# Sixteen transposes of a head in one stretch, and scores two pairs ahead instead of three, in an attention pipeline

## What is computed

```python
q, k, v = (split_heads(x @ w + b) for w, b in ((wq, bq), (wk, bk), (wv, bv)))
scores = einsum('bhqd,bhkd->bhqk', q, k) * dh ** -0.5 + adj[:, None]
ctx = einsum('bhij,bhjd->bhid', softmax(scores, -1), v)
x1 = rmsnorm(x + ctx @ wo + bo, alpha1, gamma1)
x2 = rmsnorm(x1 + silu(x1 @ w1 + b1) @ w2 + b2, alpha2, gamma2)
out = layernorm(x + x2)
```

## Time and profile before

| | before |
|---|---|
| median of 3 runs | 1987.84 us (1987.14 to 1990.58) |
| the profiled execution: its time, its span | 1988.0 us, 1986.0 us |
| busy share PE, PEld, DVE, ACT, POOL | 97%, 86%, 67%, 59%, 34% |
| mean granted TensorE clock | 0.988 |
| transposes of probabilities (L655), count, mean | 2048, 273 ns |
| `pT_hi` (L449) and `pT_lo` (L540), count, mean | 256 each, 1026 and 1225 ns |
| exponentials (L442), count, mean | 512, 712 ns |
| logits on `adj_s` (L532), count, mean | 448, 687 ns |

### The profile page before, as it was taken

One profiled execution on the slowest core, in us unless ns is written; L12 is line 12 of the kernel. 1 busy time (PEld: TensorE's weight loads), 2 busy tenths in 40 slices (PEclk: granted clock), 3 DMA queues, 4 the chain that ended last, 5 costly groups with the idle time before them and its releaser, 6 DMA issues. The chain is left out here.

```text
span 1986.0 us, 35712 instructions
## 1 busy us (share of the span) xinstructions
PE 1931.9 (97%) x10336; PEld 1703.9 (86%) x10336; DVE 1334.3 (67%) x2270; ACT 1173.4 (59%) x1896; POOL 675.2 (34%) x796
## 2 busy tenths in 40 slices
PE   7999999999999999999966999999999999999998
PEld 5888888888888888888855999999999999999997
DVE  5777777777777777777756656565666555656644
ACT  4877778777787777877745433444443344444432
POOL 2000000000000000000015667766667666566643
PEclk9999999999999999999987999999999999999999
DMA  7655565555655556455633311222221122222011
GB/s 228 146 142 151 154 181 132 142 150 155 181 130 143 149 155 183 126 145 149 158 114 106 110 60 58 81 84 84 84 83 50 44 77 84 84 84 84 18 39 40
DMA packets 107363, 226.86 MB, mean 114 GB/s; under 512 B 15041, under 2 KB 43457, under 8 KB 105281
## 3 DMA queue, kind: packets, MB, share of 16 engines
q1 hardware_dynamic: 107328, 226.43, 39.4%
HBM read 108.93 MB, written 41.94 MB: 76 GB/s over the span
## 5 line engine op out<-in xcount | busy, mean ns | idle before, releaser
L540 DVE TENSOR_TENSOR pT_lo<-ps_t,pT_hi 128x1024 fp32r<-128x1024 f32 x256 | 313.6, 1225 | 143.9 <-ACT pT_hi L449 143.9
L449 ACT ACTIVATE pT_hi<-ps_t 128x1024 fp32r<-128x1024 f32 x256 | 262.6, 1026 | 179.0 <-PE ps_t L655 177.6
L379 POOL TENSOR_TENSOR xT_lo<-xT_raw,xT_hi 128x512 fp32r<-128x512 f32 x48 | 62.3, 1300 | 853.0 <-ACT xT_hi L428 853.0
L442 ACT ACTIVATE probs<-probs,neg_max 128x512 f32<-128x512 f32 x512 | 338.9, 712 | 5.1 <-DVE neg_max L532 5.1
L532 DVE CUSTOM_DVE_ANT_0 probs<-ps_s,adj_s 128x512 f32<-128x512 f32 x448 | 291.0, 687 | 39.7 <-PE ps_s L646 32.6
L1129 DVE TENSOR_TENSOR h_lo<-hidden,h_hi 128x512 fp32r<-128x512 f32 x192 | 169.0, 881 | 169.6 <-ACT h_hi L1033 169.6
L655 PEld LDWEIGHTS ps_t<-ident,probs 128*128 128x128 f32 x2048 | 241.1, 141 | 35.7 <-issue 1.6
L655 PE MATMUL ps_t<-ident,probs 128*128 128x128 f32 x2048 | 267.2, 273 | 1.0 <-DVE pT_lo L540 1.0
L1249 PE MATMUL ps_y<-w_hi,h_hi 128*128 128x384 f32 x768 | 257.9, 336 | 0.0
L1249 PE MATMUL ps_y<-w_hi,h_lo 128*128 128x384 f32 x768 | 256.7, 334 | 0.0
L1249 PE MATMUL ps_y<-w_lo,h_hi 128*128 128x384 f32 x768 | 256.6, 334 | 0.0
(11 more groups left out here) (100 smaller groups left out, 3755.9 us busy)
## 6 DMA issues: line engine op xcount, KB each, us to landing
q_both<-stage_q SPq DMA_DIRECT2D x192, 192.0 KB, 3.9
ctx_dram<-ctx_stage SPq DMA_DIRECT2D x128, 224.0 KB
ctx_raw<-ctx_dram SPq DMA_DIRECT2D x16, 1792.0 KB, 7.2
k_hl<-stage_k SPq DMA_DIRECT2D x192, 96.0 KB, 3.2
adj_first<-in_adj SPq DMA_DIRECT2D x32, 512.0 KB, 9.3
adj_s<-in_adj SPq DMA_DIRECT2D x32, 512.0 KB, 6.0
xT_raw<-in_xT SPq DMA_DIRECT2D x16, 768.0 KB, 7.3
x<-in_x SPq DMA_DIRECT2D x16, 768.0 KB, 6.2
```

Of the source, the lines that this page charges most:

```text
L442: nc.scalar.activation(probs[:, at, :], probs[:, at, :], ACT.Exp, scale=-1.0, bias=neg_max[:, at:at + 1]).then_inc(exp_done, 1)
L449: nc.scalar.activation(pT_hi[:, h % 2, 2 * pair:2 * pair + 2, :, :], ps_t[pair][:, :, :].rearrange("p q (k i) -> p q k i", k=TT), ACT.Copy)\
L540: nc.vector.tensor_tensor(pT_lo[:, h % 2, s, :, :].rearrange("p q k i -> p (q k i)"), ps_t[pair][:, :, :].rearrange("p q n -> p (q n)"), p ...
```

## The change

The scores go two pairs ahead, and the transposes of both pairs of a head stand together in the odd step, on TensorE, with their `pT_high` on ScalarE and `pT_low` on VectorE. The even step keeps scores, logits, exponentials and `SIDE`. SyncE's and GpSimd's programs stay as they are.

```diff
-AHEAD = 3
+AHEAD = 2
...
             def batch(b, last=False):
                 for p in range(PAIRS):
-                    pT_high(b, p // 2, p % 2)
+                    for pair in (0, 1) if p % 2 else ():
+                        pT_high(b, p // 2, pair)
...
                         project_lo(batch_of(step, b), kind, t, shared_bank(step))
-                    pT_low(b, p // 2, p % 2)
+                    for pair in (0, 1) if p % 2 else ():
+                        pT_low(b, p // 2, pair)
...
                         scores(of, h, 2 * pair + 1)
-                    transpose_probs(b, p // 2, p % 2)
+                    for pair in (0, 1) if p % 2 else ():
+                        transpose_probs(b, p // 2, pair)
```

## The result

The changed kernel takes **2012.0 us** (median of 4 runs, 2009.2 to 2015.9) beside 1987.5 for the kernel before on the same chip (4 runs, 1986.6 to 1990.6): ratio 1.0122, 95% interval 1.0102 to 1.0142. It is slower by 24 us, where 2005.3 was forecast.

What follows compares the result with a forecast made beforehand. The attention phase was taken as bound by TensorE's own stream and its waits. Terms 11.2 + 3.0 + 1.7 + 3.5 - 0.8 - 1.3 = 17.3 on 1988.0 gave 2005.3 us, range 1995 to 2017.

Steps and rivals of the forecast that it cites:

- the mechanism with the largest share: The forecast's own mechanism, TensorE waiting for the score bank at step 5: 65%, with 1998 to 2012 us.
- The new wait: Step 5: TensorE waits for the score bank's chain over ScalarE and VectorE, 0.8 us per batch, +11.2 in fourteen middle batches.
- The first rival: Step 5: logits come in time if the second `pT_lo` starts before 2.5, waits vanish, 1990.9 us; 7%.
- Queues that it is moved past: SyncE's queue: later bias load delays `q1` stacking and the `xT` load by 4.5 us; both costed at nothing.
- The third rival: SyncE's queue is late, 0.5 to 1 us on each of 15 batches: 2013 to 2020 us; 16%.
- The wait of `stage_q`: ScalarE gets `q1`'s stacking late for `q2`'s high part; step 15's `pT_hi` 1.1 us late, hidden by a projection step's 1.3.
- The stream: TensorE's own stream: joining saves 0.01 us for each of 16 x 8 stretches, -1.3 us.
- First batch: First batch: two `pT_high` behind the `xT` load delay `q0` to 58.2, +3.0 us; half clock after TensorE's idling, +1.7.
- Last batch and end: Last batch: bare-step waits of 0.8 and a reciprocal wait of 2.7, +3.5 us; shorter waits at phase end, -0.8.
- the waits for `neg_max`: Sign of being right: TensorE waits at the first score matmul some 20 times, 0.6 to 0.8 us each, once per middle batch.
- a wait of over 3 us near 50: Sign of being right: one TensorE wait of over 3 us near 50, in the first batch.
- Rival 2, the clock: TensorE's clock drops in every batch beside step 5's wait, 1.7 us for each of 15 batches: 2031 us; 5%.

Runs made afterwards that it cites:

- the run with VectorE free early: Changed kernel with VectorE's second `pT_low` of a head moved behind the next even step's logits: 2002.39 us, ratio 1.0077 to the kernel before.
- the run with the later bias loads: Changed kernel with the next batch's bias loads issued in steps 12 and 13 instead of 11 and 12: 2003.77 us, ratio 1.0085 to the kernel before.
- `AHEAD` alone: Kernel before with scores two pairs ahead instead of three, each pair still transposed in its own step: 1988.06 us, ratio 1.0005.
- the joining alone: Kernel before with both pairs' transposes joined in odd steps, scores still three pairs ahead: 2009.65 us, ratio 1.0108.
- early `xT`: Changed kernel with bias loads in steps 12 and 13 and the second batch's `xT` load ahead of the first stacking: 2007.62 us, ratio 1.0099.
- the version with all bare steps' pairs in their own step: Changed kernel with bias loads in steps 12 and 13 and pairs of all steps without a projection transposed in their own steps: 1987.34 us, ratio 1.0001.

## Why the prediction was right, and where it was wrong

The side and the range were right (2012.0 in 1995 to 2017), and so was the mechanism with the largest share. The sum was 7 us short of the measured time. Term by term:

- **The new wait, 11.2 us** (0.8 in 14 batches): the traces show 0.84 each in the undelayed batches, 11.8, in step 5 as forecast, and 12 to 13 went when steps 4 and 5 alone were undone in all sixteen batches. The chain by which I timed it was also right: the logits start 4.41 after the sixteen transposes (175.64 to 180.05), the number of the prediction, and the bank is filled again at 5.15 (180.79) for a forecast of 5.25. What it left out is that this chain isn't the only one. The bank's own round trip of 1.5 us ends at the same time. The first rival's condition, an earlier second `pT_low`, would therefore not have brought its 11.2: the run with VectorE free early won 0.04 of the 0.84.
- **Queues that it is moved past, costed at nothing**: this step failed. It measured 7.9 us, and 7 to 8 by the run with the later bias loads. I had seen the chain (the bias load behind later logits, the slack of 3.6 used up by a delay of 4.5) and written that each further us is a us of TensorE; I then trusted "some idle time behind" on ScalarE, which I had not followed to the logits of step 4. The load is in fact issued 3.6 us later on average (1.4 after the first `v0` matmul, before 2.2 ahead of it), and it is wanted 0.9 earlier, since the even step's `pT_high` no longer stands before it; the prediction had missed this second half. Together they come to the 4.5 that I had forecast for the issue alone. The cover was 0.8, and seven of fourteen batches went beyond it. The third rival had this mechanism and 2013 to 2020, and its sign, `xT_hi` waiting and `pT_hi` behind it, is there; the result lies between it and the forecast, since half of the batches were late and not all. The wait of `stage_q`, forecast at 1.1 and hidden, was 0.9 at most and hidden.
- **The stream, -1.3**: joining gives 0.02 to 0.03 a batch (62.27 to 62.25 or 62.24), 0.3 to 0.4 in all. The step that failed is the difference of 0.01 between 0.88 and 0.87, read from rows of two decimals and multiplied by 128. Averaged over the middle batches, sixteen transposes take 1.67 to the next matmul, and before, eight took 0.795; with the 0.085 by which a matmul behind a stretch is late that is 1.76 either way within 0.01.
- **First batch, +3.0 and +1.7**: 4.1 measured for 4.7, by another mechanism, so the agreement is luck. ScalarE waited for `xT` only 0.28, not for the time that I had built the chain on, and `q0` came at 60.24 and not at 58.2. The rows show two waits of TensorE, each with a half clock beside it:

```profile
37.18 0.80 PE L619 MATMUL ps_g<-xT_hi,wk_hi 128*128 128x512 f32 x1 [3.60 <-DVE stage_q L510]
...
46.76 0.67 PE L646 MATMUL ps_s<-k_hl,q_both 96*128 96x512 f32 x1 [2.30 <-DVE neg_max L533]
```

```profile
36.70:40.10 3.40, 2.92 (x7) 2.34 (x8) 1.64 (x5) 1.63 (x3) 0.00 (x0) 0.50 0.56 134
46.90:50.30 3.40, 3.40 (x13) 2.88 (x14) 1.82 (x6) 1.81 (x3) 1.23 (x1) 0.50 0.98 319
```

  The first wait stands in step 0, of which I followed nothing: a pair of scores (`AHEAD`) and the transposes of pair 0 (the joining) are no longer ahead of `k2`, so TensorE arrives early. With `AHEAD` alone this wait is 2.79, with the joining alone 1.91. But `k2` begins only 0.06 later than in the old kernel, whose TensorE was busy until then:

```profile
37.12 0.49 PE L617 MATMUL ps_g<-xT_hi,wk_hi 128*128 128x512 f32 x1
```

  From `k2` to `q0` the change takes 23.06 us and the old kernel 19.87. The waits between them are about the same in sum (2.30 and 0.43 against 1.26 and 1.29), and the change has 6.8 us at half clock there and the old kernel none, so most of the 3.2 goes with the clock; that is read from the two traces, and no run removed it. Of the forecast's +3.0, the 0.93 for one more pair of scores is done only in the last batch.
- **Last batch and end, +3.5 and -0.8**: 1.3 measured for 2.7. Four waits stand there, of 0.45 to 0.48 by the view (0.6 from start to start) beside the reciprocal's 2.03, for four of 0.8 and one of 2.7; and the half clock behind the reciprocal, which I left as it was, lasted 3.4 us and not 6.8. What this is worth can be read from two versions with the same last batch: it takes 51.27 without half clock (later bias loads), 52.67 with 3.4 us (the change) and 54.07 with 6.8 (early `xT`), so 1.4 for each 3.4. With the 6.8 of the old kernel it would be 2.7, the forecast's number.

```profile
1023.28 0.80 PE L646 MATMUL ps_s<-k_hl,q_both 96*128 96x512 f32 x1 [2.03 <-DVE neg_max L533]
```

```profile
1023.10:1026.50 3.40, 3.22 (x11) 2.72 (x12) 2.14 (x8) 1.33 (x2) 0.00 (x0) 0.51 0.27 69
```

  At the end of the phase the wait of 1.01 is gone and the 0.69 stays, 1.0 less where 0.8 was forecast. Of the signs, the waits for `neg_max` are there 22 times in the whole trace, most of 0.45 to 0.48 by the view; a wait of over 3 us near 50 is not (2.30 at 46.76, 3.60 at 37.18).
- **Rival 2, the clock**: it stayed at 1.00 over the 900 us, with fourteen waits beside stretches of sixteen transposes; only after the one wait of 1.92 did it fall. The rule that the full clock doesn't engage for transposes (the Trainium skill, TensorE: Matmul & The Clock Gate, Part 4: PE-mode transpose) is not borne out as far as stretches between other matmuls go: sixteen took 1.91 at 1.00. The 1.7 for a half clock, here and in the first batch, was taken from a stretch of 3.4 us that no row of the prediction shows; the old trace has one, at 31.2 to 34.6.

Put against the sum, the forecast of 17.3 without the queue's term is close to what the run with later bias loads measured, 16.8. A part of that agreement is luck. In its profile, 15.0 us over the old one, the middle batches cost 11.8 where the wait and the stream were forecast at 10.1 for them, the first batch 4.3 for 4.7, the last nothing for 2.7, and the feed-forward phase gave 1.0 back.

## What to carry to other kernels

Before work is moved out of a step, ask what lies between two fillings of the same buffer there: if the engine's own work in between is shorter than the buffer's round trip over the other engines, the difference is a wait, whatever the order on those engines (0.60 here). Price a delay in a queue again after the change's other waits are in, since a delay that is hidden by slack is hidden only once, and the slack may be what the change spends; look also at whether the consumer now wants the data earlier. And try a new order only in the steps that can pay for it: here the same stretch of sixteen cost nothing beside a projection and 0.84 us in a bare step.

## What the runs showed of the hardware

The half clock after a wait of about 2 us comes in some executions and not in others. In the last batch, at the same instruction, a wait of 2.03 was followed by 3.4 us at half clock in the change and one of 2.06 by 6.8 us in the version with early `xT`, while one of 2.05 in the version with later bias loads was followed by none. TensorE there, and the stretch behind it at full clock:

```profile
1015.59 0.50 PE L646 MATMUL ps_s<-k_hl,q_both 96*128 96x512 f32 x1 [2.05 <-DVE neg_max L533]
```

```profile
1015.60:1019.00 3.40, 3.40 (x23) 2.84 (x24) 1.96 (x7) 2.47 (x4) 0.00 (x0) 1.00 0.24 64
```

The other one, the version with early `xT`:

```profile
1016.40 0.80 PE L648 MATMUL ps_s<-k_hl,q_both 96*128 96x512 f32 x1 [2.06 <-DVE neg_max L535]
```

```profile
1016.10:1019.50 3.40, 3.10 (x10) 2.61 (x11) 2.25 (x8) 1.33 (x2) 0.04 (x1) 0.50 0.29 72
```

In 3.4 us there were 23 matmuls at full clock and 10 at half. In the version with `AHEAD` alone even a wait of 2.79 (ahead of `k2`, at 39.03) and one of 2.33 in the last batch were followed by none, while 2.33 in the version with all bare steps' pairs in their own step was followed by 3.4 us at half clock. What decides wasn't found, and a forecast of a wait of this size carries an uncertainty of 1.4 to 2.8 us for it, by the last batches above. That may be part of why the changed kernel's four runs spread over 6.7 us, where its granted clock went from 0.986 in the slowest to 0.991 in the fastest. The load of `xT`, too, landed anywhere from 7.5 to 10.0 us after the first `v0` matmul of a middle batch, with its issue between 1.0 and 2.1; what moves the landing stays open. That landing decides which of the change's batches are late.
